# An attention step reordered: both halves of K first, single score heads between half projections, all value units at the step's end

## What is computed

```python
Q = query @ Wq.T + bq            # 16 x 100 x 256
K = key @ Wk.T + bk              # 16 x 361 x 256
V = value @ Wv.T + bv
dot = jnp.einsum('bhsd,bhtd->bhst', Q, K) / np.sqrt(D_HEAD)
scores = jax.nn.softmax(dot, axis=-1)
out = jnp.einsum('bhst,bhtd->bhsd', scores, V)
return out.reshape(B, T_src, D_MODEL) @ Wh.T + bh
...
x = x + jnp.tanh(g_xattn[0]) * attention(layernorm(x), ctx, ctx)
x = x + jnp.tanh(g_ffn[0]) * experts(layernorm(x))
```

## Time and profile before

| | |
|---|---|
| time of the profiled execution | 538.21 us |
| its span | 536.4 us |
| PE busy | 512.6 us (96%) |
| PEld (weight loads) busy | 465.6 us (87%) |
| DVE (VectorE) busy | 351.5 us (66%) |
| ACT (ScalarE) busy | 259.4 us (48%) |
| POOL (GpSimd) busy | 293.3 us (55%) |
| chain that ended last | PE 81%, DMA 8%, DVE 6%, ACT 3% |
| of it, DMA QS<-crow | 6% |

### The profile page before, as it was taken

How to read it: one execution, slowest core, us unless ns; L and a number is a source line. 1 busy time by engine, 2 the same in 40 slices (tenths; PEclk the granted TensorE clock), 3 DMA queues, 4 the chain that set the end, 5 groups by cost and what they waited for, 6 DMA issues and landing times.

```text
span 536.4 us, 11868 instructions
## 1 busy us (share of the span) xinstructions
PE 512.6 (96%) x4392; PEld 465.6 (87%) x4392; DVE 351.5 (66%) x774; ACT 259.4 (48%) x578; POOL 293.3 (55%) x339
## 2 busy tenths in 40 slices
PE   8879899999899999999998999999999999999995
PEld 6658698888788888788788999999999999999993
DVE  5857577777677777787756777765476555754443
ACT  4457446555455555556757523353335333343331
POOL 6474446665455456552549964844367433944441
PEclk9999999999999999999989989999999999999998
DMA  6774766776676777765111000000000100001000
GB/s 213 194 229 130 193 175 152 180 179 156 138 172 164 175 174 188 162 140 114 19 17 17 0 1 2 1 1 31 2 2 0 32 1 0 2 0 32 1 0 31
DMA packets 50888, 45.83 MB, mean 85 GB/s; under 512 B 33967, under 2 KB 40275, under 8 KB 50832
## 3 DMA queue, kind: packets, MB, share of 16 engines
q1 hardware_dynamic: 40782, 20.92, 16.9%
q0 software_dynamic: 6704, 15.93, 12.4%
q10 hardware_dynamic: 3346, 8.23, 5.3%
HBM read 20.59 MB, written 6.66 MB: 51 GB/s over the span
## 4 chain that ended last, share of the span: by engine, by line
PE 81%; DMA 8%; DVE 6%; ACT 3%; issue 2%; POOL 1%; SPq 0%; POOLq 0%; DVEq 0%; ACTq 0%
PE bank L1315 13%; PE bank L1177 9%; PE bank L1194 7%; PE bank L1207 7%; PE bank L1367 6%; PE bank L1319 6%; PE bank L1332 6%; DMA QS<-crow 6%; PE bank L1160 5%; PE bank L1347 4%; PE bank L1152 3%; PE bank L1240 2%; PE bank L1350 2%; DMA xs<-x 2%; PE bank L1281 2%
## 5 line engine op out<-in xcount | busy, mean ns | idle before, releaser
L922 DVE TENSOR_REDUCE nmax<-bank 100x1 f32<-100x361 f32 x256 | 128.1, 527 | 56.1 <-PE bank L1177 52.8
L408 POOL TENSOR_TENSOR awl<-hb,awh 128x400 fp32r<-128x400 f32 x64 | 71.9, 1125 | 101.6 <-ACT awh L616 101.6
L517 ACT ACTIVATE pt<-bank 120x400 f32<-120x400 f32 (+1 forms) x192 | 82.7, 504 | 26.1 <-PE bank L1194 25.8
L1177 PE MATMUL bank<-KS,QS 96*100 96x362 f32 x256 | 89.8, 385 | 4.4 <-DVE nmax L922 3.9
L616 ACT ACTIVATE awh<-hb 128x400 fp32r<-128x400 f32 x64 | 34.5, 539 | 118.4 <-DVE hb L868 118.2
L861 DVE TENSOR_TENSOR hb<-sil,bank 128x400 f32<-128x400 f32 x64 | 36.5, 570 | 83.7 <-PE bank L1332 39.4
L344 POOL DMA_DIRECT2D KS<-kn x64 | 32.6, 517 | 96.9 <-PE bank L1177 52.7
L1177 PEld LDWEIGHTS bank<-KS,QS 96*100 96x100 f32 x256 | 42.1, 166 | 24.0 <-issue 12.9
L1194 PE MATMUL bank<-QS,KS 97*120 97x200 f32 (+1 forms) x384 | 51.4, 270 | 4.4 <-DMA QS<-crow 3.8
L1194 PEld LDWEIGHTS bank<-QS,KS 97*120 97x120 f32 (+1 forms) x384 | 49.0, 185 | 6.8 <-DMA QS<-crow 6.1
L868 DVE TENSOR_TENSOR hb<-hb,wbT 128x400 f32<-128x400 f32 x64 | 46.0, 718 | 2.1
(11 more groups left out here) (185 smaller groups left out, 1134.0 us busy)
## 6 DMA issues: line engine op xcount, KB each, us to landing
KS<-kn SPq DMA_DIRECT2D x128, 90.5 KB, 2.9
KS<-kn POOLq DMA_DIRECT2D x64, 90.5 KB, 2.8
craw<-ctxT POOLq DMA_DIRECT2D x14, 361.0 KB, 6.5
QS<-q_dram POOLq DMA_DIRECT2D x92, 50.0 KB, 5.3
q_dram<-qn ACTq DMA_DIRECT2D x4, 400.0 KB, 5.6
o_dram<-on SPq DMA_DIRECT2D x16, 100.0 KB
xr<-o_dram SPq DMA_DIRECT2D x16, 100.0 KB
y<-xs SPq DMA_DIRECT2D x16, 100.0 KB
```

What stands on the lines that cost most here:

```text
L408: nc.gpsimd.tensor_tensor(awl[:, g % 2, slot], hb[:, slot], awh[:, g % 2, slot].bitcast(F32), ALU.subtract).then_inc(m["p_awl"], 1)
L517: nc.scalar.activation(pt[0:TW[t], u % 6, :], pT[u % 3][0:TW[t], 0:CS], ACT.Exp, scale=float(DH) ** -0.5).then_inc(m["act_e"], 1)
L922: nc.vector.tensor_reduce(nmax[:, pos:pos + 1], pS[h % 2][0:S, 0:T], AX.X, ALU.max, negate=True).then_inc(m["dve_s"], 1)
L1177: mm(pS[h % 2][0:S, 0:TP], QS[b % 3][0:96, g, h % 2, j, :], KS[b % 3][0:96, g, j, :], start=True, stop=True).then_inc(m["pe_s"], 1)
```

## The change

No arithmetic is added or removed. On TensorE, in each step but the last:

- `row_turn` of half 1 comes first in the step instead of behind three st units, three pv units and two heads.
- K's halves (0, then 1) come first, and V's parts follow. Each projection is cut into two halves of three matmuls, with a single head between them.
- All 12 pv units stand together at the end of the step, behind head 15. The last step keeps its groups of three.

ScalarE, VectorE and SyncE follow: `row_out` of half 1 is ScalarE's first work in the step, both `k_high` come in a row, `row_out` of half 0 stands behind `v_out` of part 1; both `k_low` come earlier; `root` (small operations on VectorE in steps 11 and 12) moves from between the heads to behind head 15. The orders on SyncE and GpSimd are the same as before. `pt` gets 12 buffers, so that `expo` waits for the pv unit of the batch before.

Before, L500 stood behind L636 and the two L487 were apart. The diff, cut to its core:

```diff
-        pt = sba("pt", [121, 6, CS])
+        pt = sba("pt", [121, UN, CS])
...
-                wait(act, "pe_pv", n - 5)
-                nc.scalar.activation(pt[0:TW[t], u % 6, :], pT[u % 3][0:TW[t], 0:CS], ACT.Exp,
+                wait(act, "pe_pv", n - UN + 1)
+                nc.scalar.activation(pt[0:TW[t], u, :], pT[u % 3][0:TW[t], 0:CS], ACT.Exp,
...
+            def k_part(b, j, p0, p1):
+                for p in range(p0, p1):
+                    (hw, hc), k = TERMS[p // KT], p % KT
+                    last = mm(pP[(1, 0)[j]][:, 0:TP], wkv[:, 0, hw, k, j * 128:(j + 1) * 128],
+                              cth[:, b % 2, hc, k, :], start=p == 0, stop=p == 5)
+                if p1 == 6:
+                    last.then_inc(m["pe_k"], 1)
...
             def body(i):
                 b = i + 2
-                if has_u(i):
-                    st_unit(i, 0)
-                    st_unit(i, 1)
-                    st_unit(i, 2)
-                if has_o(i):
-                    pv_unit(i - 1, 9)
-                    pv_unit(i - 1, 10)
-                    pv_unit(i - 1, 11)
+                wait(pe, "act_v", min(NT * (i + 2), NT * B))
+                wait(pe, "act_c", 2 * i)
+                row_turn(i, 1)
+                st_unit(i, 0)
+                st_unit(i, 1)
+                st_unit(i, 2)
                 if has_s(i):
                     s_head(i + 1, 0)
-                    s_head(i + 1, 1)
...
+                    k_part(b, 0, 0, 3)
+                if has_s(i):
+                    s_head(i + 1, 1)
+                if has_k(i):
+                    k_part(b, 0, 3, 6)
                 if has_s(i):
                     s_head(i + 1, 2)
+                if has_k(i):
+                    wait(pe, "act_c", 2 * i + 2)
+                    k_part(b, 1, 0, 3)
+                if has_s(i):
                     s_head(i + 1, 3)
                 if has_k(i):
-                    wait(pe, "act_c", 2 * i + 2)
-                    v_proj(b, 0)
+                    k_part(b, 1, 3, 6)
...
                 if has_s(i):
-                    s_head(i + 1, 14)
                     s_head(i + 1, 15)
+                    pv_unit(i, 0)
+                    pv_unit(i, 1)
...
+                    pv_unit(i, 10)
+                    pv_unit(i, 11)
```

More of the change, by code:

```diff
@@ L636, in body @@
                     nc.scalar.activation(osb[:].rearrange("p q s -> p (q s)"), pO[:, 0:CS], ACT.Copy).then_inc(m["act_o"], 1)
-                if has_u(i):
-                    row_out(i, 1)
                 if has_k(i):
                     k_high(b, 0)
-                    wait(act, "pe_pv", i * UN)
-                    v_out(b, 0)
+                    k_high(b, 1)
                 if i == B - 2:
@@ L651, in body @@
                 if has_k(i):
-                    k_high(b, 1)
+                    wait(act, "pe_pv", i * UN)
+                    v_out(b, 0)
                 if i == B - 2:
@@ L983, in body @@
                     head(i + 1, 1)
-                if i in (11, 12):
-                    root(0, 7 * (i - 11))
+                    head(i + 1, 2)
+                if has_k(i):
+                    k_low(b, 0)
                 if has_s(i):
-                    head(i + 1, 2)
                     head(i + 1, 3)
-                if i in (11, 12):
-                    root(0, 7 * (i - 11) + 1)
-                if has_s(i):
                     head(i + 1, 4)
                 if has_k(i):
-                    k_low(b, 0)
+                    k_low(b, 1)
                 if has_s(i):
@@ L1050, in body @@
                     variance(i - 3)
+                if has_s(i):
+                    head(i + 1, 15)
+                if i in (11, 12):
+                    for k in range(7 * (i - 11), 7 * (i - 11) + 6):
+                        root(0, k)
                 if i == 11:
                     root(0, 6)
-                if has_s(i):
-                    head(i + 1, 14)
-                    head(i + 1, 15)
             for i in range(0, B):
@@ L1149, in k_proj, with v_part @@
                     pe.wait_ge(m["ctx_l"], b + 1)
[L1150 to L1154, removed]
+                k_part(b, j, 0, 6)
+            def k_part(b, j, p0, p1):
[5 more added lines that the diff above has]
+                    last.then_inc(m["pe_k"], 1)
             def v_proj(b, t):
+                v_part(b, t, 0, 6)
+            def v_part(b, t, p0, p1):
                 bank = (pS[0], pS[1], pT[2])[t] if b == 0 else pP[1] if b == 1 and t == 1 else pP[0]
[L1158 to L1162, removed]
+                for p in range(p0, p1):
+                    (hw, hc), k = TERMS[p // KT], p % KT
+                    last = mm(bank[0:TW[t], 0:D], cth[:, b % 2, hc, k, T0[t]:T0[t] + TW[t]],
+                              wkv[:, 1, hw, k, :], start=p == 0, stop=p == 5)
+                if p1 == 6:
+                    last.then_inc(m["pe_v"], 1)
             def s_head(b, h):
@@ L1509, in body @@
                 if has_s(i):
-                    s_head(i + 1, 8)
+                    s_head(i + 1, 9)
+                if has_k(i):
+                    wait(pe, "act_v", NT * b + 1)
+                    v_part(b, 1, 0, 3)
+                if has_s(i):
+                    s_head(i + 1, 10)
+                if has_k(i):
+                    v_part(b, 1, 3, 6)
+                if has_s(i):
                     if has_o(i):
@@ L1515, in body @@
                     row_turn(i + 1, 0)
[L1516 to L1521 removed]
+                    s_head(i + 1, 11)
                 if i == B - 2:
```

98 lines of the change are left out of this document (46 added, 52 removed).

## The result

The changed kernel takes **532.75 us** in the median of 16 runs (526.14 to 536.64). The kernel before took 536.34 in 16 runs beside it (533.53 to 541.66). The ratio is 0.9903, with a 95% interval of 0.9874 to 0.9932. So the kernel is about 5 us faster by the ratio (3.6 by the medians), where 15 were forecast. The time lies inside the range, near its upper end.

The account below looks back on a forecast made before the run. TensorE was taken to set the pace. A step of 13.21 + 0.2 + 0.6 = 14.0 us against 15.10, over 14 steps, saves 15.3: 538.2 - 15.3 = 523 us, own range 517 to 529, with neighbours 514 to 535.

Parts of the forecast that it names:

- One pv block instead of four, -1.03: On TensorE, three times the 0.34 us paid around a pv block goes away, saving 1.03 us a step.
- The rival at block pace: The pv run keeps the pace of a block: only 0.55 saved, 14.5 us a step, 530 us; chance 0.08.
- Heads 0 and 1, -0.38: At a step's start, VectorE has finished head 15 by then, so heads 0 and 1 save 0.38 us a step.
- VectorE, +0.2: Single heads between half projections, tight from head 3 to head 10: 0.2 us a step added, from 0 to 0.5.
- 13.21: TensorE's issue work in one step, us: 14.62 less 1.03 for pv blocks and 0.38 for heads 0 and 1.
- The rival in which VectorE paces the step: Waits at the heads and head 0 stay: 14.7 us a step, 533 us; chance 0.10.
- Row store half 1, +0.6: Waits for the landing of half 1's row of maxima add 0.6 us a step, from 0.3 to 1.7.
- I cost step 14, 15 and the rest at nothing, within 1 us: Steps 14 and 15 and the rest of the kernel change nothing, within 1 us either way.
- The row store eats the gain: Half 1 lands 7.0 us after issue every step, behind K's DMAs: 15.0 us a step, 537 us; chance 0.13.
- Half 0 is late too: Half 0's row store also lands late for st unit 0: 16.0 us a step, 551 us; chance 0.05 (slower).

Follow-up runs that it names:

- e8: Changed kernel without the row store of half 1 and its waits, pv units in groups of three as before; 545.98 us, ratio 1.017 to the kernel before.
- e7: Kernel before without the row store of half 1, its 12 pv units in one go behind head 15; 529.91 us, ratio 0.987.
- e1: Changed kernel with the row store of half 1 and the waits for it left out; 524.34 us, ratio 0.977 to the kernel before.
- e2: Kernel before with the row store of half 1 and the waits for it left out; 533.44 us, ratio 0.993.
- e3: Changed kernel with the row store of half 1 issued by ScalarE instead of SyncE; 531.89 us, ratio 0.989 to the kernel before.
- e5: Changed kernel with row_turn of half 1 ahead of the pv run, its store ahead of K's last two DMAs; 526.44 us, ratio 0.982 to the kernel before.
- e6: e5 with GpSimd's context load moved behind K's remainder DMAs; 531.53 us, ratio 0.988 to the kernel before.
- e9: e5 with row_turn of step 0 behind st unit 2 and step 14's pv units in groups of three; 526.86 us, ratio 0.980 to the kernel before.
- e10: e9 with V's last part between heads 13, 14 and 15; 529.28 us, ratio 0.982 to the kernel before.
- e11: Changed kernel with ten throwaway transpositions of the identity ahead of the wait for half 1; 538.54 us, ratio 1.002 to the kernel before.
- e4: Changed kernel with GpSimd's context load moved behind K's remainder DMAs, mid-step; 529.11 us, ratio 0.981 to the kernel before.

## Why the prediction came out as it did

- **One pv block instead of four, -1.03: right.** The run's weight loads, the row of after that answers to the earlier trace rows:

```profile
178.56 2.04 PEld L1203 LDWEIGHTS bank<-pt,va 121*17 121x17 f32 x96 [0.30 <-issue]
```

  2.04 / 96 = 0.0213 each, forecast 0.020. From the run's start to the next row it is 2.20, a little over the 1.9 to 2.1 named and well under the 2.5 that would have refuted it. e8 gives 0.9 for three switches. The rival at block pace falls.
- **Heads 0 and 1, -0.38, and VectorE, +0.2: right.** DVE stood still for 1.90 us before head 0's reduction, and no head at the start waited:

```profile
181.85 1.86 DVE L921 TENSOR_REDUCE nmax<-bank 100x1 f32<-100x361 f32 x3 [1.90 <-PE bank L1173]
```

  The quiet step is 13.48 to 13.49, against 13.21 + 0.2 = 13.41. Waits on nmax add up to 3.6, under the 5 named. The rival in which VectorE paces the step falls, for this order; e7 shows it is the order that keeps it away.
- **Row store half 1, +0.6: the wait was right, the term was not.** 8.4 / 14 = 0.60 us of weight loads held up. That it meets the figure to the digit is luck: the prediction chose it between 0.3 and 1.7, and thought of many small waits, where three of the eight made 5.8 of the 8.4. SyncE's rows answer to the earlier trace rows:

```profile
149.07 1.60 SPq L242 DMA_DIRECT2D QS<-crow  x1
...
176.89 3.78 SPq L238 DMA_DIRECT2D KS<-kn  x6
...
181.31 0.67 SPq L242 DMA_DIRECT2D QS<-crow  x1
```

  The store at 149.07 released PE at 156.82, 7.75 later; its issue alone took 1.60 instead of 0.67, so here 0.9 was lost in SyncE's queue. The forecast let 7.0 be the worst. **This is the step that failed:** it priced a late store at the time that PE stands still. It left out the lower clock that followed three of the long standstills, and it had no term for K, whose own DMAs land after 4.0 instead of 2.9 and held up heads. That denser traffic delays them is my reading (DMA share 0.73 against 0.69). In the profile these are 6.9 and 1.65 us, so 0.49 and 0.12 a step: 13.48 + 0.60 + 0.49 + 0.12 = 14.69, measured 14.65. Before carried a clock loss of 1.7 in its own 15.10, unseen in the prediction. It put the whole 0.48 above the quiet step down to waits, though rows at the lower clock follow its longest wait (at 64.35, 1.69 of the 3.8 us of the earlier trace rows).
- **"I cost step 14, 15 and the rest at nothing, within 1 us": wrong in the profile** (+3.0 at the start, -1.7 at the end), mostly by the clock, which fell before step 0 in after (0.96 over 42 us) and in e1, e2, e3, e5, e6, e7, e9, e10 and e11, and not in before, e4 and e8. The steady part is `row_turn` of step 0, 0.8 us.
- **Rivals.** "The row store eats the gain" is the nearest, by another road: it had each store late by 1.6; in fact six steps are undisturbed and three are very long (17.18, 16.56, 18.76). "Half 0 is late too" did not happen, no wait stood at st unit 0 in a step; it did in e4 and e6, where the context load was moved.

**Over all runs the clock weighs less than in the one profile.** The median is 9.7 us above the 523 of the forecast. The forecast still held 5.3 us of clock loss (before's profile lost 7.0, of which 1.7 in the 14 steps), and the runs lost 9.0, so 3.7 of the 9.7 are clock. Another 5.2 are in the profile, which makes this an estimate: K's landing 1.65, the quiet step 13.48 instead of 13.41 (1.0), the start of step 0 beyond its clock (1.3), the experts (0.4), and 14 steps of before that are 210.6 us from st group to st group where the prediction took 211.4 (0.8). So terms put at nothing (K, the start, the experts) weigh about as much as the clock.

At full clock the change is worth 7.8 us of 15.3: half 1 takes 522.9 - 517.2 = 5.7 after and 530.7 - 526.4 = 4.3 before, and the 2.1 of clock come on top. Taking half 1 out of both leaves 9.2 at full clock, where 14 quiet steps differ by 16; the 14 steps of e1 and e2 differ by 13.7, and the ends take back the rest (start +2.2, steps 14 and 15 +2.6, clock in part, experts +1.0, in one profile each).

Open: what exactly delays half 1. It is not the issuing queue (e3); it goes with what else is under way (e4 to e6), but none of the runs singles out K or Q; of the context e4 shows that its place sets about half of the waits for half 1. Open too is why some waits of over 1 us were followed by the lower clock and others not.

## What to carry over

Before you tighten a step whose transfers already have little room, read how late the latest of them would be, not the mean: three late stores of 14 made 12 of the 16 us above the quiet steps, about half of it the waits (5.8) and half the lower clock behind them (6.8). Where an edit frees time on the bounding engine, spend some of it on moving the start of the tightest transfer ahead (e5: 0.44 a step longer, every wait for it gone, 5 to 6 us faster and less scatter). And compare runs with their clock beside them; a single profile here was up to 5 us off for that alone (e4's lost 1.6 us to the clock, its ten runs 6.5 in the mean).

## What the runs showed of the hardware

- **A wait of 1.2 to 1.9 us can be followed by some 3 to 7 us at the lower clock, whatever was waited for.** It was so after waits for a DMA (66.59, 125.25, 156.82), and in e2 after a wait for VectorE:

```profile
219.37 0.75 PE L1175 MATMUL bank<-KS,QS 96*100 96x362 f32 x2 [1.42 <-DVE nmax L920]
...
220.04 1.94 PE L1150 MATMUL bank<-cth,wkv 128*128 128x362 f32 x6
```

  Six K matmuls take 1.94 there, 1.16 in the earlier trace rows. It does not always follow. After a wait of 1.27 for K in after, three matmuls took 0.52 as ever:

```profile
109.88 0.41 PE L1173 MATMUL bank<-KS,QS 96*100 96x362 f32 x1 [1.27 <-DMA KS<-kn]
...
111.14 0.52 PE L1155 MATMUL bank<-wkv,cth 128*120 128x256 f32 x3
```

  The 14 steps of the 13 profiles hold 14 waits of PE of 1.17 us or more for a DMA or for VectorE. Six were followed by the lower clock and eight were not, among them the longest of all (1.95 in e4, clock 1.00 over its 14 steps). In no case did the clock fall in these steps without such a wait at most 2.3 us before. So a long wait goes ahead of the lower clock, but does not foretell it.

- **Small matmuls in column strips take 0.0213 us each,** 96 in a row. In the single records of the run the four of a unit, one in each strip, start 5 to 8 ns apart, and the next four some 66 ns after them. The Trainium skill (TensorE: Matmul & The Clock Gate, Part 1: The HAM clock gate) gives a floor of about 25 ns from start to start however small a matmul is; the four of a unit go below it, and there the measurement decides.
- **Cutting a projection in two costs nothing:** three matmuls of K and a head take 0.66 to 0.67 each time, as the prediction had it from six.
